# Cross attention of a transformer block: ScalarE's third exponential of a step placed before the eviction of the step's projection

## What is computed

```python
q_c = _ln(x) @ W_qc + b_qc
kv_c = _ln(context) @ W_kvc + b_kvc
k_c, v_c = jnp.split(kv_c, 2, axis=-1)
c_attn_w = jax.nn.softmax(jnp.einsum('bhqd,bhsd->bhqs', q_c, k_c) * scale, axis=-1)
c_attn_out = jnp.einsum('bhqs,bhsd->bhqd', c_attn_w, v_c)
```

## Time and profile before

| | us |
|---|---|
| median of 3 runs (2734.64 to 2736.46) | 2734.68 |
| the profiled execution | 2742.2 |
| its span, first to last instruction | 2740.1 |
| TensorE busy | 2641.8 (96%) |
| VectorE busy | 1718.8 (63%) |
| GpSimd busy | 1296.6 (47%) |
| ScalarE busy | 1133.7 (41%) |

### The profile page before, as it was taken

The page is one execution under the profiler, slowest core; times in us unless marked ns, Lnnn a source line. Parts: engine busy times, 40 slices in busy tenths (PEclk is TensorE's granted clock), DMA queues, the critical chain, the costliest instruction groups (busy, mean ns, idle before and its releaser), DMA issues. The chain is left out here.

```text
span 2740.1 us, 50012 instructions
## 1 busy us (share of the span) xinstructions
PE 2641.8 (96%) x18612; PEld 2155.5 (79%) x18612; DVE 1718.8 (63%) x3477; ACT 1133.7 (41%) x2187; POOL 1296.6 (47%) x1447
## 2 busy tenths in 40 slices
PE   8999999999879999999999999999889999999997
PEld 6688888888668888888888888887568888888886
DVE  6677777777727777677776777666654444444431
ACT  4345444444434555555555555554532112122110
POOL 1444445454414777777677777777710220220211
PEclk9999999999789999999999999999899999999999
DMA  8454444545343444444444444433331111111110
GB/s 222 130 129 117 125 127 122 133 109 144 100 125 95 111 109 108 113 114 114 110 108 118 117 109 107 116 94 97 109 113 35 43 47 36 43 47 35 43 43 23
DMA packets 170769, 269.86 MB, mean 98 GB/s; under 512 B 30849, under 2 KB 84609, under 8 KB 170513
## 3 DMA queue, kind: packets, MB, share of 16 engines
q1 hardware_dynamic: 167456, 259.33, 35.3%
q0 software_dynamic: 3072, 7.34, 0.8%
HBM read 111.11 MB, written 36.77 MB: 54 GB/s over the span
## 5 line engine op out<-in xcount | busy, mean ns | idle before, releaser
L1630 ACT ACTIVATE cross_prT<-cross_tr_ps 125x448 f32<-125x448 f32 x768 | 405.9, 544 | 298.8 <-PE cross_tr_ps L1391 289.8
L1510 DVE TENSOR_REDUCE cross_parts<-cross_sc_ps 112x1 f32<-112x500 f32 x512 | 337.6, 664 | 244.2 <-PE cross_sc_ps L1377 243.0
L1677 POOL TENSOR_TENSOR cross_part<-cross_prT 125x448 f32<-125x448 f32 x252 | 291.1, 1155 | 219.3 <-PE cross_or_ps L1411 130.8
L1017 POOL TENSOR_TENSOR self_psum<-self_prT 112x224 f32<-112x224 f32 x256 | 173.3, 677 | 352.4 <-ACT self_prT L907 343.1
L1391 PE MATMUL cross_tr_ps<-cross_qst,cross_kst 98*125 98x224 f32 x1536 | 313.3, 289 | 10.6 <-ACT cross_prT L1630 6.5
L1391 PEld LDWEIGHTS cross_tr_ps<-cross_qst,cross_kst 98*125 98x125 f32 x1536 | 254.3, 189 | 79.9 <-ACT cross_prT L1630 33.8
L1679 POOL TENSOR_TENSOR cross_part<-cross_part,cross_prT 125x448 f32<-125x448 f32 x252 | 292.6, 1161 | 19.8
L2074 ACT ACTIVATE mlp_hv<-mlp_h_ps,mlp_b 128x512 f32<-128x512 f32 x112 | 76.9, 687 | 520.1 <-PE mlp_h_ps L73 506.1
L1377 PE MATMUL cross_sc_ps<-cross_kst,cross_qst 96*112 96x500 f32 (+1 forms) x1024 | 266.0, 339 | 5.0 <-DVE cross_parts L1510 3.1
L1991 DVE CAST mlp_hT_h<-mlp_hv 128x512 fp32r<-128x512 f32 x112 | 53.0, 473 | 320.8 <-ACT mlp_hv L2074 320.8
L907 ACT ACTIVATE self_prT<-self_st_ps 112x448 f32<-112x448 f32 x256 | 138.9, 543 | 212.8 <-PE self_st_ps L487 211.5
(11 more groups left out here) (275 smaller groups left out, 6766.7 us busy)
## 6 DMA issues: line engine op xcount, KB each, us to landing
cross_kst<-cross_nat_h SPq DMA_DIRECT2D x512, 93.8 KB, 2.2
cross_c_in<-in_context SPq DMA_DIRECT2D x96, 250.0 KB
cross_kst<-cross_nat_l SPq DMA_DIRECT2D x256, 93.8 KB, 2.2
cross_qst<-qc SPq DMA_DIRECT2D x192, 112.0 KB, 2.5
self_kst<-self_nat_h SPq DMA_DIRECT2D x128, 112.0 KB, 2.3
self_qst<-self_natq_h SPq DMA_DIRECT2D x128, 112.0 KB, 3.3
self_x_in<-in_x SPq DMA_DIRECT2D x16, 448.0 KB, 3.7
self_kst<-self_nat_l SPq DMA_DIRECT2D x64, 112.0 KB, 2.3
```

What stands on the lines that cost most here:

```text
L1017: pool.tensor_tensor(psum[:, j], prT[:, j, 0], prT[:, j, 1], ALU.add).then_inc(p_summed, 1)
L1510: dve.tensor_reduce(parts[:, g % 2, j, u, 0:1], sc_ps[u][0:QN, 0:SHALF[0]], AX_X, ALU.max, negate=True).then_inc(maxed, 1)
L1630: act.activation(prT[:, slot(h), 2 * c:2 * c + 2], bank(h, c)[0:SN, 0:2 * N].rearrange("p (k t) -> p k t", k=2), ACT.Exp).then_inc(exped, 1)
L1677: pool.tensor_tensor(part[:], prT[:, j, 0:2], prT[:, j, 2:4], ALU.add).then_inc(pre_summed, 1)
```

## The change

On ScalarE, in steps 0 to 14, the eviction of a K or V piece is issued after the step's third exponential and no longer between the second and the third. Context pieces keep their place: behind both in steps 11 to 14, ahead of the third exponential in step 15. The other engines' code is not touched.

```diff
             def body(b, att, nxt, prv):
                 for h in range(NH):
                     for c in range(ST // 2):
-                        for f, o in fill_at(b, h, "kv" if h < NH - 1 else "c") if c == 2 else ():
+                        for f, o in fill_at(b, h, "c") if c == 2 and h == NH - 1 else ():
                             high(o, f)
                         for o, l in late(b, h, att, prv):
                             exps(o, l, c)
+                    for f, o in fill_at(b, h, "kv"):
+                        high(o, f)
                     for f, o in fill_at(b, h, "c") if h < NH - 1 else ():
                         high(o, f)
```

## The result

| | before | after |
|---|---|---|
| median of 7 runs each, us | 2735.17 (2734.64 to 2736.88) | 2744.57 (2741.36 to 2746.62) |
| ratio after to before, 95% interval | | 1.0031 [1.0020, 1.0042] |
| the profiled execution, us | 2742.2 | 2745.4 |
| its span, us | 2740.1 | 2743.4 |

The changed kernel is 9.4 us slower; 8.9 were forecast. The two profiled executions differ by only 3.2 us, because that of before was a long one. It enters the cross attention's loop 2.8 us later than the one of after, in a part of the program that the change doesn't touch. So I compare inside the loop, from one V or K piece's first weight load to the same one of the other trace: there the changed kernel loses 6.5 us between step 7 of round 0 and step 14 of round 14.

The account below looks back on a forecast made before the run. TensorE was taken to set the pace. V waits of 7.6 us plus 1.3 in round 14, with 0 for K evictions and step 6, gave +8.9 on 2734.7, so 2743.6 us; 8-in-10 range 2736.5 to 2747.

Parts of the forecast that it names:

- The V waits: Steps 13, 14: TensorE's loads wait for later V copies, 0.26 and 0.28 us in rounds 0-13, 0.65 in round 14.
- The place: Even PSUM bank: only V4's and V5's loads wait, for V3's and V4's copies; all other V copies have cover.
- K evictions hidden: K steps: the later eviction still ends before VectorE's subtraction, some 0.37 us of cover; counted as 0 us.
- Step 6: TensorE's 0.21 us wait for ScalarE goes, but the wait for VectorE's row maximum grows to about 0.6; value 0.
- The 0.36 gaps: TensorE's waits behind 32-column P.V matmuls: a fixed cost of leaving narrow matmuls, not waits for ScalarE, so unchanged.
- the faster rival: Gaps after row sums and step 6's wait shrink with earlier exponentials, V copies free: -9.9 us, 2724.8; chance 0.05.
- I take nothing back: Waits after the V copies hang on chains starting at TensorE and move with it, so none of 8.9 us returns.

Follow-up runs that it names:

- the three kernels above: Kernel before with step 5's normalisation behind the third row maximum (0.9991), step 5's K eviction behind step 6's first exponential (1.0005), or both (0.9993).

## Why the prediction was right, and where it wasn't

- **The V waits, the term that decides.** Forecast 0.26 and 0.28 us in rounds 0 to 13, 0.65 twice in round 14, 8.9 in all. The trace has 0.26 and 0.28 in every one of rounds 0 to 13, and 0.65 and 0.63 in round 14: 4.33 + 4.55 = 8.9 us. The chain was built of start spacings rather than durations. The copy starts 0.44 us after the exponential (0.43 taken) although that lasts 0.54; adding durations would have made each wait 0.1 us too long. That no other V copy matters is shown by moving all but these two (0.9999).
- **The place.** Only steps 12 and 13 wait, since the context pieces in between put V3, V4 and V5 in one bank. Moving these two alone costs +7.0 us; delaying them further costs +27.9.
- **K evictions hidden.** Moved alone, 1.0000. The same K piece as in the earlier trace rows, timeline of after:

```profile
905.87 0.38 PE L1391 MATMUL cross_tr_ps<-cross_qst,cross_kst 98*125 98x224 f32 x2
...
906.73 0.57 ACT L1613 ACTIVATE cross_nat_h<-cross_even_ps,cross_bkv 128x376 fp32r<-128x376 f32 x1
...
907.69 0.60 DVE L1503 SCALAR_TENSOR_TENSOR cross_nat_l<-cross_even_ps,cross_bkv,cross_nat_h 128x376 fp32r<-128x376 f32 x1
```

The eviction ends at 907.30, and the subtraction starts at 907.69, 0.39 us later; by the forecast's times it was 909.87 - 909.46 = 0.41. From the third pair to the subtraction it is 1.82 us, where the earlier trace rows has 909.87 - 908.04 = 1.83: nothing moved.

- **Step 6.** The value, 0, was right, and the reason (VectorE's row maximum comes last) is shown by the three kernels above. One number of it was wrong. The forecast had TensorE's load of the third pair at 1422.30 on the clock of before; it came at 1421.92, which is 1421.92 + 0.36 = 1422.28 there. But the wait for VectorE was to grow to 0.6, as if that load had not moved. It waits 0.51 us itself, for step 6's first exponential, so VectorE's share shrinks to 0.24. Only the end, 2.53 us behind the third pair, stays.
- **The 0.36 gaps.** They did not move: 14 x 0.51 + 41 x 0.36 = 21.9 is the whole of the line of 21.8 above, though the exponentials ahead of them came up to 0.25 us earlier. Had they followed ScalarE, the line named ScalarE would have shrunk. The same 0.36 stands before the context pieces that follow 32-column products (9.3 / 26, the `cross_odd_ps` line named "issue"), which need no exponential. With that the faster rival falls. The cause of the gap itself, the change of matmul shape, was argued and not tried.
- **"I take nothing back".** This step failed. I reasoned that all later waits hang on chains that start at TensorE. The placed maxima don't: they come through SyncE's queue behind 500 KB of context tiles, and are late now and then in any kernel (1.0 to 2.3 us a run in the profiled kernels that keep the order of before on SyncE and don't hold up V4 and V5). With the V waits ahead of them TensorE comes later and finds them there: 0.3 us left in the changed kernel, none in the two with only steps 12 and 13 moved. So 8.9 become about 6.5 in the profiled loop.

Why then 9.4 us by the medians, and 7.0 and 6.9 in the two later comparisons, of the kernels that move V3 and V4 alone and of the changed kernel with SyncE's edit? The intervals are +-3 us wide, so all of them fit 6.5 as well as 8.9. The forecast's 8.9 lacks a term of about -2, and it is luck that the first measurement came out so close to it.

How large the term is depends on the execution, since which rounds have such a wait differs from one to the next. Step 2 costs 2.6 us more in the profiled run of before than where no such wait is left; in the five other profiled kernels that have SyncE's old order and don't hold up V4 and V5 it is 1.4 to 2.5. The average of the six is 2.0 us, that of the three kernels that hold them up 0.2. That gives an estimate of -1.9 for the term and 8.9 - 1.9 = 7.0 for the whole change.

Nor does the queue simply follow TensorE. It sets out from step 13's third pair, which stands ahead of V5's wait. Before, below after, round 7:

```profile
1386.84 1.29 SPq L1265 DMA_DIRECT2D cross_qst<-qc  x3
```

```profile
1386.21 1.27 SPq L1265 DMA_DIRECT2D cross_qst<-qc  x3
```

Both stand 1.59 to 1.60 us behind the third pair (1385.24 and 1384.62), while V5's load has moved from 1.21 to 1.48. Measured from step 12's third pair, ahead of both V waits, TensorE without its wait comes to the maxima after 23.2 us before and 23.7 after. The last maxima land after 23.0 us on average in both (rounds 0 to 12; 22.2 to 23.9 before, 22.1 to 24.1 after). So TensorE gets the 0.5 us of the V waits as a cushion, and of the six waits of before only two (0.53 and 0.72) were longer than that. The landing stays put for two reasons that cancel: the issue ends 0.3 us later, and the DMA then takes 4.5 us where it took 4.85. Why it is quicker stays open.

## What to carry to other kernels

On an in-order engine, moving one instruction ahead moves another back; ask first which PSUM bank the one moved back releases, and how long it is until that bank is filled again, and build the new time from start spacings of the trace. A wait on the busiest engine is worth only what the next wait behind it leaves: at step 6 ScalarE's wait was visible, VectorE's was the price. Look also at what arrives by a path of its own (here a DMA behind large loads): it can absorb a part of a loss. Here its waits went away when its queue was reordered, in the trace (-2.6 us in the loop); the medians can't tell that gain from none by itself.

## What the runs showed of the hardware

- In the changed kernel ScalarE starts a PSUM copy 0.44 us after the start of an exponential of 448 columns that lasts 0.54, and an exponential 0.46 us after a K eviction that lasts 0.57 (0.47 in the kernel before). TensorE's load that waits for the copy starts 0.05 us after the copy's end, at all 30 places of the changed kernel.
- The gap of 0.36 us when TensorE leaves 32-column products, in 41 waits named ScalarE, 41 or 42 named "issue" and 26 more ahead of context pieces, doesn't depend on when the named releaser is done.
- A DMA of 3.5 KB issued behind 500 KB on the same queue landed 4.6 to 5.4 us after the end of its issue in the kernel before; with the large ones behind it, 1.1 to 2.3 us, and TensorE never waited for it.
